# Cross-attention values for all sequences as ten 128-row chunks through DRAM, and a new order of the first layer's queues

## The reference

```python
# first attention: 16 heads of 8, with relative positions
Q, K, V = x @ Wq + bq, x @ Wk + bk, x @ Wv + bv
scores = Q.K / sqrt(8) + einsum('bhid,ijd->bhij', Q, rel_table[rel_idx])
# cross-attention: 16 heads of 64
q = x @ Wq;  k = context @ Wk;  v = context @ Wv      # v: 77 rows of 1024 for each sequence
sim  = einsum('bihd,bjhd->bhij', q, k) * 64 ** -0.5
out  = einsum('bhij,bjhd->bihd', softmax(sim), v).reshape(B, N, 1024) @ Wo
```

## Time and profile before

| | |
|---|---|
| median of 3 runs | 760.82 us (757.53 to 761.97) |
| profiled execution, its own time | 759.91 us |
| its span in the trace | 758.1 us |
| mean granted TensorE clock | 0.972 of full |
| first layer | about 0 to 400 us |
| TensorE / VectorE / ScalarE / GpSimd busy | 676.5 / 551.8 / 403.4 / 206.8 us |

### The profile page before, as it was taken

How to read it: one execution, slowest core, us unless ns; L and a number is a source line. 1 busy time by engine, 2 the same in 40 slices (tenths; PEclk the granted TensorE clock), 3 DMA queues, 4 the chain that set the end, 5 groups by cost and what they waited for, 6 DMA issues and landing times.

```text
span 758.1 us, 21348 instructions
## 1 busy us (share of the span) xinstructions
PE 676.5 (89%) x8334; PEld 519.2 (68%) x8334; DVE 551.8 (73%) x2013; ACT 403.4 (53%) x1172; POOL 206.8 (27%) x212
## 2 busy tenths in 40 slices
...
GB/s 347 255 264 207 161 134 171 171 171 167 158 166 126 125 172 178 235 145 18 22 101 69 33 32 9 10 11 13 15 13 13 14 13 14 16 12 13 5 6 7
DMA packets 48259, 72.22 MB, mean 95 GB/s; under 512 B 2832, under 2 KB 43280, under 8 KB 45472
## 3 DMA queue, kind: packets, MB, share of 16 engines
...
## 4 chain that ended last, share of the span: by engine, by line
PE 57%; DVE 23%; issue 9%; ACT 8%; DMA 2%; another core or an unknown queue 1%; POOL 1%; SPq 0%; DVEq 0%; ACTq 0%
PE bank L559 47%; PE bank L620 4%; PE bank L705 3%; DVE k L1662 3%; DVE scol L1704 2%; ACT kbd L1209 1%; ACT kbd L1210 1%; DVE nmb L1346 1%; DMA xT_ld<-xT 1%; DVE k L1640 1%; DVE kbd L1754 1%; DVE q L1731 1%; DVE y_d L1678 1%; ACT pTb L1104 1%
## 5 line engine op out<-in xcount | busy, mean ns | idle before, releaser
L1065 ACT ACTIVATE sc<-sc,nmxa 128x128 f32<-128x128 f32 x256 | 79.5, 390 | 34.9 <-DVE nmxa L1289 34.9
L498 POOL TENSOR_TENSOR early<-early,recb 128x616 f32<-128x616 f32 x32 | 38.9, 1217 | 187.9 <-DVE recb L1377 187.9
L1289 DVE CUSTOM_DVE_ANT_0 sc<-bank,rel 128x128 f32<-128x128 f32 x256 | 56.4, 286 | 14.7 <-PE bank L559 14.3
L1662 DVE TENSOR_TENSOR k<-bank,k_sb 128x512 f32<-128x512 f32 x64 | 41.1, 684 | 29.7 <-PE bank L559 21.0
L1299 DVE COPY pTa<-bank 128x512 f32<-128x512 f32 x32 | 22.0, 689 | 32.7 <-PE bank L620 32.7
L559 PE MATMUL bank<-k,xdT 128*128 128x512 f32 x96 | 45.5, 610 | 0.0
L1045 ACT ACTIVATE rext<-bank 128x512 f32<-128x512 f32 x64 | 34.7, 609 | 18.0 <-PE bank L559 18.0
L475 POOL TENSOR_TENSOR rext<-rext,ones 128x1008 f32<-128x1008 f32 x16 | 29.9, 1869 | 52.9 <-ACT rext L1045 52.8
L534 POOL TENSOR_TENSOR oTb<-x_all,row_sb 128x128 f32<-128x128 f32 x16 | 7.3, 458 | 133.8 <-DVE pTa L1683 133.8
L1112 ACT ACTIVATE early<-early 128x308 f32<-128x308 f32 x64 | 27.3, 452 | 29.8 <-DVE early L1362 29.8
L620 PE MATMUL bank<-k_sb,sc 128*128 128x128 f32 x256 | 36.6, 289 | 7.3 <-issue 6.5
...
## 6 DMA issues: line engine op xcount, KB each, us to landing
rel_dram<-rext SPq DMA_DIRECT2D x16, 2040.0 KB, 7.2
rel<-rel_dram SPq DMA_DIRECT2D x16, 960.0 KB, 5.6
...
```

The source lines that it names most:

```text
L498: G.tensor_tensor(pB[:, part, :], pB[:, part, :], recb[:, part].unsqueeze(2).broadcast_to([P, 8, C]), ALU.mult).then_inc(b_even, 1)
L1065: last = A.activation(sc[:, h, :], sc[:, h, :], ACT.Exp, bias=nmxa[:, h:h + 1], scale=-1.0)
L1289: last = V.tensor_tensor_reduce(out=sc[:, h, :], in0=bank[i][:, a * P:(a + 1) * P], in1=rel[:, t % 2, h, :], scale=-1.0, scalar=FAR, op0=A ...
L1662: V.tensor_tensor(scd[:, 4 * i:4 * i + 4, :], bank[(1, 2, 0, 1)[i]][:].rearrange("p (a t) -> p a t", a=4), const("causal").unsqueeze(1).br ...
```

## The change

Values are made for chunks of 128 rows of all contexts together, ten chunks (the last of 80 rows). Chunks 0 to 3 are made early (`v_early(0)` and `v_early(1)`, in rounds -2 and -1, four matmuls each, all copied by VectorE); chunks 4 to 9 in rounds 0, 2, 4, 6, 8, 10, at the place of `v0`, one half copied by ScalarE, one by VectorE. Each chunk is stored from `vs` to the DRAM tensor `v_dram`, and for each sequence 77 rows of 4 KB are loaded from there into one of two buffers `v0`. All stores and loads are on SP's queue. `keys(0)` moves ahead of `a_s(0)`, and `keys(1)` between `a_t1(0)` and `a_t2(0)`. In VectorE's order `b_norm` moves behind `a_t3`, `a_add`, `a_st`, `a_ag` ahead of `b_sum0`, and the routing steps `r_s`, `r_p0` behind `b_rec1`. The tail lists name only steps that still have to be done, and their order is changed in a few places. The zeros for `xg_dram` come from `pTb`, later. ScalarE issues four of its loads after `xT_ld[0]` has landed. In the second layer, chains of three semaphores become one.

```diff
+CHUNKS_EARLY = ((0, 1), (2, 3))
+CHUNK_AT = {0: 4, 2: 5, 4: 6, 6: 7, 8: 8, 10: 9}
+EARLY = 2 * sum(len(part) for part in CHUNKS_EARLY)
 ORDER1 = {
-    "pe": ("a_t2:1 a_t3:1 b_t1:-1 b_t2:-1 b_t3:-1 a_s:2 keys:2 b_q a_v:1 b_s0 b_s1 a_qkv:4 b_v0:-1 b_v1:-1 "
-            "a_out:1 b_out:-1 rel_last:4 b_r:-2 v0 b_lg:-2 rel:4 b_x:1 a_t0:2 a_t1:2 r_rank:-3 b_t0").split(),
-    "dve": ("a_t3 b_t1:-2 b_t3:-2 a_m0:1 b_qhi:-1 a_m1:1 b_m0:-1 b_m1:-1 b_l0:-1 b_m2:-1 b_l1:-1 b_l2:-1 a_div "
-            "b_norm:-3 b_u0:-2 b_m3:-1 b_u1:-2 a_qkv:3 b_l3:-1 b_sum0:-1 a_add b_rec0:-1 a_st rel_last:3 "
-            "b_add:-2 a_ag b_sum1:-1 a_ln r_p1:-4 r_n:-5 b_lg:-3 r_w:-19 r_a:-3 r_b:-4 b_st:-2 r_s:-3 r_p0:-3 "
-            "b_rec1:-1 b_ag:-2 v0:-1 a_t1:1 r_rows:-4 r_c:-4").split(),
+    "pe": ("a_t3:1 b_t1:-1 b_t2:-1 b_t3:-1 a_s:2 b_q v_early:2 a_v:1 b_s0 b_s1 a_qkv:4 b_v0:-1 b_v1:-1 a_out:1 "
+            "b_out:-1 rel_last:4 v0 b_r:-2 rel:4 b_lg:-2 b_x:1 a_t0:2 a_t1:2 keys:3 r_rank:-3 b_t0 a_t2:2").split(),
+    "dve": ("a_t3 b_norm:-3 b_t1:-2 b_t3:-2 a_m0:1 b_qhi:-1 a_m1:1 b_m0:-1 b_m1:-1 b_l0:-1 b_m2:-1 b_l1:-1 v_early:1 "
+            "b_l2:-1 a_div b_u0:-2 b_m3:-1 b_u1:-2 a_qkv:3 a_add b_l3:-1 a_st rel_last:3 a_ag r_p1:-4 b_sum0:-1 "
+            "b_rec0:-1 a_ln b_sum1:-1 r_b:-4 b_lg:-3 b_add:-2 r_w:-20 r_a:-3 b_st:-2 b_rec1:-1 r_n:-5 b_ag:-2 v0:-1 "
+            "r_s:-3 a_t1:1 r_rows:-4 r_c:-4 r_p0:-3").split(),
...
-    "sp": "load_rel:5 store_rel:6".split(),
+    "sp": "v_early:4 store_rel:6 v_late:2 v_load:4 load_rel:6".split(),
...
+            def store_late(t):
+                if t in CHUNK_AT:
+                    sp.wait_ge(v_lo, chunks_late(t))
+                    sp.wait_ge(v_hi, EARLY + chunks_late(t))
+                    store_chunk(CHUNK_AT[t])
+            def load_v(t):
+                last = ((t + 1) * C - 1) // P
+                for i in range(2):
+                    need(sp, st_v[i], 16 * ((last + 2 - i) // 2))
+                need(sp, values["b"], 2 * (t - 1))
+                sp.dma_start(v0[t % 2][0:C, :, :].rearrange("p h d -> p (h d)"), v_dram[t * C:(t + 1) * C]
+                             ).then_inc(ld_v[t % 2], 16)
...
+            def early_values(t):
...
+                for n in CHUNKS_EARLY[t]:
+                    for i in range(2):
...
+                        mm(bank[4 + (h + 1) % 4][0:P, :], cTf[:, n * P:(n + 1) * P], w("c0_wv", i * 512, (i + 1) * 512)
+                           ).then_inc(v_ps, 1)
...
-                    mm(bank[4 if i else 6][0:C, :], cT[:, t, :], w("c0_wv", i * 512, (i + 1) * 512)).then_inc(v_ps, 1)
+                    mm(bank[4 if i else 6][0:k, :], cTf[:, n * P:n * P + k], w("c0_wv", i * 512, (i + 1) * 512)
+                       ).then_inc(v_ps, 1)
...
-            keys(0, 12)
+            keys(0, 6)
             a_qkv_(1)
-            keys(12, 14)
+            keys(6, 8)
             rel_last(1)
+            keys(8, 12)
             rel_scores(1)
-            keys(14, 18)
+            keys(12, 18)
...
             A.dma_start(wk, w_k).then_inc(ld_keys, 16)
+            act.preload_act_table_set("natural_log_exp_and_others")
+            act.wait_ge(ld_xT[0], 16)
             A.dma_start(k_sb[:], consts).then_inc(ld_c, 16)
...
+            pool.wait_ge(pre_pool, 8)
+            pool.wait_ge(ld_rel[1], 32)
+            G.dma_start(xg_dram[0:SLOTS].rearrange("(n p) d -> p n d", p=P), pTb[:, 0:2 * E, :]).then_inc(st_zero, 16)
```

More of the change, by code:

```diff
@@ L88 @@
 TAIL1 = {
[12 rows of a table removed]
-            "a_v:11 a_v:12 b_x:10 a_t3:12 b_t0:12 keys:15").split(),
[23 rows of a table removed]
-            "a_t1:12 b_u0:11 r_rows:8 b_u1:11 b_ag:10 a_t3:12 r_w:6 b_norm:8").split(),
[10 rows of a table removed]
[L136 to L140, removed]
[3 rows of a table added]
+            "b_out:15 b_r:14 b_lg:14 b_r:15 b_lg:15 r_rank:14 r_rank:15").split(),
[11 rows of a table added]
+            "r_w:11 r_p0:15 r_n:14 r_p1:15 r_b:15 r_rows:14 r_c:14 r_w:14 r_rows:15 r_c:15 r_w:6 r_w:15 r_a:11 r_b:11").split(),
+    "act": "b_r:14 r_a:14 b_ln:15 b_r:15 r_a:15".split(),
+    "pool": ("r_send:5 r_send:6 b_n0:15 b_n1:15 r_send:7 r_send:8 r_send:9 r_send:10 r_send:11 r_send:12 r_send:13 "
+            "r_send:14 r_send:15").split(),
+    "sp": ("").split(),
 }
 ORDER2 = {
-    "pe": ("v1 f_turn:-2 e_out:-1 d_qk:1 e_x d_gv:1 f_down:-2 e_q d_rank:1 f_x:-1 e_s f_up:-1 e_nm d_s01:1 "
-            "e_st d_s3:1 e_inj d_v:1 d_out:1 e_v d_x:2").split(),
[3 rows of a table removed]
-            "d_gate:2 d_q:2 e_m0:1 e_m1:1 e_m2:1 e_m3:1 d_k:2 d_m0:2 d_m1:2").split(),
-    "act": ("e_e2 d_v:1 e_e3 c_ln:2 d_ln:1 e_v d_x:2 d_ln2:1 f_turn:-1 e_ln e_x:1 d_gates:2 e_q:1 f_ln:-1 f_x "
-            "d_sig:2 e_nm:1 f_exp f_sig e_e0:1 e_e1:1").split(),
+    "pe": ("v1 f_turn:-2 e_out:-1 d_qk:1 e_x d_gv:1 f_down:-2 e_q d_rank:1 f_x:-1 e_s f_up:-1 e_nm d_s01:1 e_st "
+            "d_s3:1 e_inj d_v:1 d_out:1 e_v d_x:2").split(),
[3 rows of a table added]
+            "e_m1:1 e_m2:1 e_m3:1 d_k:2 d_m0:2 d_m1:2").split(),
+    "act": ("e_e2 d_v:1 e_e3 c_ln:2 d_ln:1 e_v d_x:2 d_ln2:1 f_turn:-1 e_ln e_x:1 d_gates:2 e_q:1 f_ln:-1 f_x d_sig:2 "
+            "e_nm:1 f_exp f_sig e_e0:1 e_e1:1").split(),
     "pool": "gather:2 e_res d_res:2 d_fade:2".split(),
@@ L178, in decoder @@
 def decoder(nc, x_in, xT_in, cT_in, w_a, w_k, w_b, w_l, w_f, w_up, w_down, columns, rows, conv, consts, out,
-            rel_dram, xg_dram, yg_dram):
+            rel_dram, xg_dram, yg_dram, v_dram):
     with ExitStack() as ctx:
@@ L243, in decoder @@
         rb = early[:, 0:XC * P].rearrange("p (c i) -> p c i", c=XC)
-        v0 = sb("v0", [P, H, XH])
+        v0 = [sb(f"v0{i}", [P, H, XH]) for i in range(2)]
+        vs = [sb(f"vs{i}", [P, H * XH]) for i in range(2)]
         nmxa = sb("nmxa", [P, H])
@@ L365, in decoder @@
         v_ps, v_lo, v_hi = sem("v_ps"), sem("v_lo"), sem("v_hi")
+        st_v, ld_v = ([sem(f"{n}{i}") for i in range(2)] for n in ("st_v", "ld_v"))
         logits, lg_sb = sem("logits"), sem("lg_sb")
@@ L423, in load_rel, with store_chunk, store_early @@
                 sp.dma_start(rel[:, t % 2, H - 1, :], skewed[:, (H - 1) * M:(H - 1) * M + P]).then_inc(ld_rel[t % 2], 16)
-            run(ORDER1["sp"], {"store_rel": store_rel, "load_rel": load_rel}, BEGUN1, UNTIL1, TAIL1["sp"])
+            def store_chunk(n):
+                k = chunk_rows(n)
+                sp.dma_start(v_dram[n * P:n * P + k], vs[n % 2][0:k, :]).then_inc(st_v[n % 2], 16)
+            def store_early(t):
+                if t < len(CHUNKS_EARLY):
+                    for n in CHUNKS_EARLY[t]:
+                        sp.wait_ge(v_hi, 2 * n + 2)
+                        store_chunk(n)
+            def store_late(t):
[10 more added lines that the diff above has]
+                             ).then_inc(ld_v[t % 2], 16)
+            run(ORDER1["sp"], {"store_rel": store_rel, "load_rel": load_rel, "v_early": store_early, "v_late": store_late,
+                               "v_load": load_v}, BEGUN1, UNTIL1, TAIL1["sp"])
             sp.wait_ge(st_rel, 16 * B)
@@ L602, in last_keys @@
                     keys(18 + 3 * t, 21 + 3 * t)
+            def early_values(t):
+                if t >= len(CHUNKS_EARLY):
+                    return
+                if t == 0:
+                    pe.wait_ge(ld_wb, 16)
+                for n in CHUNKS_EARLY[t]:
+                    for i in range(2):
+                        h = 2 * n + i
+                        if t == 0 and h < 3:
+                            pe.wait_ge(k0_sb, 18 + h)
+                        elif t == 0:
+                            pe.wait_ge(k0_sb, 21)
+                        else:
+                            pe.wait_ge(k0_sb, 3 * XC)
+                            pe.wait_ge(v_hi, 4)
+                        mm(bank[4 + (h + 1) % 4][0:P, :], cTf[:, n * P:(n + 1) * P], w("c0_wv", i * 512, (i + 1) * 512)
+                           ).then_inc(v_ps, 1)
             def a_scores(t):
@@ L746, in b_out, with late_values @@
                 last.then_inc(proj["b"], 1)
-            def v0_(t):
-                if t == 0:
-                    pe.wait_ge(ld_wb, 16)
-                    pe.wait_ge(k0_sb, 3 * XC)
+            def late_values(t):
+                if t not in CHUNK_AT:
+                    return
+                n, k = CHUNK_AT[t], chunk_rows(CHUNK_AT[t])
                 for i in range(2):
@@ L1117, in f @@
                     act.wait_ge(turned, 4 * t + i + 1)
+                    if t == 0:
+                        act.wait_ge(st_zero, 32)
                     need(act, values["b"], 2 * (t - 1) + 1 + i // 2)
@@ L1121, in b_turn, with late_values @@
                 return f
-            def v0_(t):
-                act.wait_ge(v_ps, 2 * t + 1)
-                A.activation(v0[0:C, 0:8, :], bank[6][0:C, :].rearrange("p (h d) -> p h d", d=XH), ACT.Copy
-                             ).then_inc(v_lo, 1)
+            def late_values(t):
+                if t not in CHUNK_AT:
```

(36 more changed lines are left out.)

71 lines of the change are left out of this document (39 added, 32 removed), and 65 rows, old and new, of tables (ORDER2, TAIL1).

## The result

Over 20 runs each the changed kernel has a median of 762.60 us (758.45 to 766.57), the kernel before 759.54 (757.53 to 762.77); the ratio is 1.0041, with a 95% interval of 1.0024 to 1.0058. That lies within the 0.5% that the prediction counted as no change, where I forecast 752.0 and a faster kernel. A second comparison on another chip gave 761.28 against 758.82, 1.0039 (1.0011 to 1.0067). The profiled execution took 762.33 us with a span of 760.5, 2.4 more than before; it should have been 8.9 less.

The account below looks back on a forecast made before the run. The prediction took TensorE to set the first layer's steady rounds. Rounds -13.7, prologue +5.0 and start -0.2 summed to -8.9 us, so 752 from a median of 760.82, with a range of 744 to 760.

Parts of the forecast that it names:

- Round 10 keeps its chunk, but the routing steps no longer stand ahead of `b_rec1`: 0.6: Round 10, first layer: moving the routing steps on VectorE gains 0.6 us, between 0 and 0.85.
- the 1.5 gained in round 9: Round 9, first layer, set by VectorE: it comes to 19.7 us, so 1.5 gained.
- The 1.6 of a round without `v0`: First-layer rounds without value matmuls: TensorE loses 1.75 us of work, 0.15 is lost to a late `x<-y_a`, 1.6 gained.
- Rounds 11 and 12: First layer, rounds without value matmuls: gains of 1.6 us and of 1.0, the latter between 0.65 and 1.6.
- The 5.0 us of the prologue: Rounds -2 and -1: four early chunks add 7.0 us of TensorE work, two absorbed by waits; +5, bounds +2 and +14.
- The "clock stays up" rival: Prologue, 38 to 50 us: added matmuls keep the clock at 2.4 GHz, 4 us come back, 748; chance 0.12.
- Round 1: First layer: 1.6 us gained without `v0`; its 3 us excess length at clock 0.92 was not addressed.
- the stalls that move: Unexplained stalls in the tail and round 1 shift: gone 743, one more 757 to 761; chance 0.06.
- VectorE as the bound: Rounds 1, 3, 5, 7, 9, 11 give half as VectorE limits them: 4.6 us less gain, 756.5; chance 0.14.
- `load_rel` late: SP queue: value loads delay `load_rel`, so `a_m0` starts late in 11 rounds; 759.6 to 783, slower; chance 0.10.
- The tail: From `a_s(15)` on: 2.6 us less forecast.
- The sum: Whole kernel: -13.7 + 5.0 - 0.2 = -8.9 us, giving 752.

Follow-up runs that it names:

- the two order edits: Changed kernel with the send ahead of `rel_fill` on GpSimd and `r_s`, `r_p0` behind `b_st` on VectorE, as before: 753.53 us, side by side 753.55.
- With the gap filled: Changed kernel with both old orders restored, plus eight unread 256-column matmuls in TensorE's prologue wait ahead of `rel_last(2)`: 752.15 us, 0.9923.
- The kernel before with the collision put in: Kernel before, no chunks, with `rel_fill` ahead of the send, `r_s` behind `v0` and `r_p0` behind `r_c`: 768.04 us, 1.0115.

## Why the prediction was wrong

*The step that failed* is "Round 10 keeps its chunk, but the routing steps no longer stand ahead of `b_rec1`: 0.6", with the 1.5 gained in round 9. I priced the move by what it freed, and never asked what runs on GpSimd where the steps land, nor what an earlier `b_rec1` starts there. In place of gains of 1.5 and 0.6 us came losses of 1.6 and 4.1: VectorE's products ran beside `rel_fill`, were held until it ended, and TensorE waited and then ran at a lower clock. Taking back the two order edits gives 1.9 in round 9 and 4.2 in round 10, and 7.7 us in the median measured side by side (761.28 to 753.55; the two rounds place 6.1 of them by the first pair of traces, and rounds 9 to 11 differ by 8.5 in the side-by-side pair). Even so round 9 is then 20.83 against 21.16 before: its missing chunk gave 0.3 and not 1.5, and no run here shows what bounds it.

*GpSimd's list* I did not price at all: the swap of the send and `rel_fill` isn't in the prediction. Alone it is worth 3.3 us of median (761.28 to 758.00) or 4.6 (from 762.60), of which 2.5 are in round 10.

*The 1.6 of a round without `v0`* measured 1.2 to 1.3 (rounds 3, 5, 7), and putting the matmuls back in rounds 3 and 5 costs the same 1.25. The mechanism was right, the size not: the trip `rel_last` - copy - `rel`, not `x<-y_a`, is what comes late next. Rounds 11 and 12 have 0.8 and 0.7 for 1.6 and 1.0.

*The 5.0 us of the prologue*, which I trusted least, came as 5.6 in the first trace. In the nine traces with this prologue `a_s(2)` starts at 66.35 to 68.69, so 3.5 to 5.9 later than before, and the agreement is partly luck. I also stopped the account at `a_s(2)`. In round 0 of the first trace TensorE ran at the lower clock for some 7 us (my estimate from its mean of 0.84 over 20.88 us); `v0` took 3.76 instead of 1.9, and round 0 20.88 instead of 18.13: 2.8 more. Five of the nine traces have that stretch and four have not, so round 0 is a chance that I had not priced. With the gap filled `a_s(2)` was 2.2 to 4.5 us earlier than in any of the nine: that part of the prologue's price is clock and not work. The "clock stays up" rival had its condition wrong: more matmuls alone did not hold the clock (0.66 at 40 to 50), since they left the gap of 2.73 us in front of `rel_last(2)`. Its price of 4 us is not shown: the median moved by 1.4, inside the noise.

*Round 1* gave 4.4 for 1.6, as a dip of the clock to 0.92 in it was gone. I had left it among the stalls that move. The kernel before with the collision put in has the dip too (22.42, 0.92), and none of the kernels with chunks has it in this round. No run shows what removes it.

*VectorE as the bound*: no. It is busy 15.90 of 18.36 us, and took no part in the extra matmuls' 1.25. (Half of the gain of the rival's six rounds is 4.75 us, not 4.6.)

*`load_rel` late*: no. In round 5 the value load is issued at 175.30, `rel` at 176.43, and `a_m0` still waits for TensorE; in all of the first layer VectorE waits once for this load, for 0.6 us. The issue of `rel` is 11.1 us into the round, against 8.7 before: 2.5 later where I had 1.8, and the slack carried it.

*The tail*: -2.6 forecast, -2.6 measured. This one agreement is worth little: that stretch spread from 429.6 to 442.1 us over the profiled executions of these kernels.

*The sum.* With the two moves undone the median is 753.5, close to 752.0. It isn't the forecast coming true: round 9 and the short rounds give less, the clock costs more where its low stretch falls in round 0, and round 1 gives back more, than I had in it.
